# Graph layer with gathered rows: gather indices for eight blocks in one transfer, in a ring of 16 blocks

## The chip, the core and the metric

The kernel runs on one core of a Trainium2 chip. The core has TensorE (PE, with its weight loads PEld), VectorE (DVE), ScalarE (ACT), GpSimd (POOL), SyncE (SP) and 16 DMA engines. The metric is the time of one execution on the device in microseconds (us); less is better.

## The reference, cut to what matters

A message-passing layer over 12,500 nodes (64 features) and 412,500 edges, sorted by destination:

```python
h = relu(layernorm(x))
h0 = pe_val @ W0 + b0                      # pe_val: 32 features per edge
t  = gelu(h0) @ W1 + b1
h0 = h0 + (gelu(t) @ W2 + b2)
score = h0 @ W3 + b3                       # 64 per edge
msg  = h[src] * score                      # h[src]: the gather
sums = segment_sum(msg, dst); cnt = segment_sum(1, dst)
out  = x + (sums / max(cnt, 1)) @ Wo + bo
```

## The kernel before

Edges are padded to 403 blocks (`NB`) of 1024 edges, each block 8 tiles (`TILES`) of 128. Setup computes the layer norm of x and writes it to DRAM (`h_rows`), loads the weights, and prepares a table of destinations. Then every engine walks over the blocks in its own loop; semaphores alone order the engines among each other.

For block b, with buffers picked by parity (a for even b, b for odd b) or by ring:

- **SP** issues loads four blocks ahead: `pair` (the edge features for the first product) once `h0_done` says that block b's first product is over, `act_in` (the same features for the last product) once `score_done` says that block b's last product is over. Then, for block b + 8, it waits on `gathered` of block b and issues the load of the gather indices `idx` (L221, one block: 128 partitions of 8 numbers, 4 KB). SP works strictly in order, so the index load of block b + 8 stands behind the wait for `score_done` of block b.
- **POOL** runs `gather_ahead`: wait for `msg_done` of block b (the slot of `rows` is free again), wait for `idx_in` of the slot, then eight indirect DMAs (L309), each of which fetches 128 rows of `h_rows` into `rows`. So POOL may be at most 8 blocks (`G_RING`) ahead.
- **PE** per block, in this order in `steps`: `second(b)` (L404, ps_h1), `first(b+1)` (L398, ps_h0, signals `h0_done`), `sums(b-1)` (L422, ps_w, after `msg_done` of b-1), `last(b)` (L413, ps_s, signals `score_done`). The names ps_sa and ps_sb tell even blocks from odd ones.
- **ACT** applies gelu twice: `g` from ps_h0 (L353), then `act_in` from ps_h1 (L358).
- **DVE** builds the one-hot tile (L574), then `message(b)` (L582) multiplies ps_s with `rows` after it has waited for `score_done` and `gathered` of block b, signals `msg_done`, and adds a window of sums into `acc` (L684).

The wait of POOL on the indices and the load that answers it are:

```python
slot = s % G_RING
pool.wait_ge(idx_in[slot], uses(b, G_RING) * 16)
...
sp.wait_ge(gathered[s % G_RING], uses(b, G_RING) * 16 * TILES)
load_idx(b + G_RING, s + G_RING)
```

Of the kernel before, what the change touches and what calls it, by code (L numbers as in the profile page):

```python
# [22 lines left out]
I32 = mybir.dt.int32  # L23
# [4 lines left out]
P = 128  # L28
# [4 lines left out]
TILES = 8  # L33
HALF = TILES // 2 * P
BLOCK = TILES * P
NB = -(-E // BLOCK)
# [12 lines left out]
G_RING = 8  # L49
IN_RING = 4  # L50
# [18 lines left out]
def edge_gated_layer(nc, x, edges, src, dst, dst_rows, weights, out):  # L69

    with ExitStack() as ctx:
        def sb(name, shape, dt=F32):
            return ctx.enter_context(nc.sbuf_tensor(name, shape, dt))
# [4 lines left out]
        def sem(name):  # L78
            return ctx.enter_context(nc.semaphore(name))
# [32 lines left out]
        iota_i = sb("iota_i", [P, WIN], I32)  # L112
        iota = sb("iota", [P, WIN])

        idx = sb("idx", [P, G_RING, TILES], I32)
        pair = sb("pair", [2 * DE, IN_RING, HALF])
        act_in = sb("act_in", [D + DE + 1, IN_RING, 2, HALF])
        g1 = sb("g1", [P, 2, HALF])
# [38 lines left out]

        pair_in = [sem(f"pair_in{s}") for s in range(IN_RING)]
        attr_in = [sem(f"attr_in{s}") for s in range(IN_RING)]
        idx_in = [sem(f"idx_in{s}") for s in range(G_RING)]  # L160
        gathered = [sem(f"gathered{s}") for s in range(G_RING)]
        h0_done = sem("h0_done")
        g1_done = sem("g1_done")
# [6 lines left out]
        msg_done = sem("msg_done")  # L170
# [25 lines left out]
        def blocks_loop(eng, first, end, unroll, step):  # L196

            turns = (end - first) // unroll
            if turns < 2:
                turns = 0  # L200
            else:
                with eng.Fori(0, turns) as i:
                    for u in range(unroll):
                        step(i * unroll + (first + u), first + u)
            for b in range(first + turns * unroll, end):
                step(b, b)

        def uses(b, ring):

            return (b >> ring.bit_length() - 1) + 1  # L210

        def tiles_of(b):
            return LAST_TILES if isinstance(b, int) and b == NB - 1 else TILES
# [3 lines left out]

        @block.sync
        def _(sp):
            def load_idx(b, s):  # L220
                sp.dma_start(idx[:, s % G_RING, :], src[one(b), :, :].rearrange("o p t -> p (o t)")  # L221
                             ).then_inc(idx_in[s % G_RING], 16)

            def load_pair(b, s):
                sp.dma_start(pair[:, s % IN_RING, :],
                             edges[one(b), :, :, :].rearrange("o g f j -> (o g f) j")
                             ).then_inc(pair_in[s % IN_RING], 16)

            def load_attr(b, s):
                sp.dma_start(act_in[D:D + DE, s % IN_RING, :, :],  # L230
                             edges[one(b), :, :, :].rearrange("o g f j -> f (o g) j")
                             ).then_inc(attr_in[s % IN_RING], 16)

            load_idx(0, 0)
            load_idx(1, 1)
            for c in range(LN_STEPS):
                cols = slice(c * LN_ROWS, (c + 1) * LN_ROWS)
                sp.dma_start(xs[:, cols, :], x_nodes[:, cols, :]).then_inc(x_in[c], 16)
            for b in range(2, G_RING):
                load_idx(b, b)  # L240
            sp.dma_start(wp[:, :], weights).then_inc(weights_in, 16)
            for b in range(2):
                load_pair(b, b)
                load_attr(b, b)
            sp.dma_start(dst_i[:, :, :], dst).then_inc(dst_in, 16)
            for c in range(CHUNKS):
                n = len(range(c, NB, CHUNKS))
                if c >= 2:

                    sp.wait_ge(bounds_step, 1 + 2 * (c - 1))  # L250
                sp.dma_start(rows_i[0:n, c % 2, :], dst_rows[c:NB:CHUNKS, :]
                             ).then_inc(rows_in[c % 2], 16)
            for b in range(2, IN_RING):
                load_pair(b, b)
                load_attr(b, b)
            sp.dma_start(x_late[:, :, :], x[N_EARLY:N, :].rearrange("(t p) d -> p t d", p=NP)
                         ).then_inc(x_late_in, 16)

            sp.wait_ge(bounds_step, 1 + 2 * CHUNKS)
            sp.dma_start(bounds_dram.rearrange("m (p c) -> p m c", p=P), bounds[:, :, :]  # L260
                         ).then_inc(bounds_out, 16)
            sp.wait_ge(bounds_out, 16)
            sp.dma_start(base_b[:, :], bounds_dram[0:1, 0:NB].broadcast_to([P, NB])
                         ).then_inc(base_in, 16)
            sp.dma_start(top[:, :], bounds_dram[1:2, 0:NB]).then_inc(base_in, 16)

            def ahead(b, s):

                sp.wait_ge(h0_done, b + 1)
                load_pair(b + IN_RING, s + IN_RING)  # L270

                sp.wait_ge(score_done, b + 1)
                load_attr(b + IN_RING, s + IN_RING)

            def ahead_all(b, s):
                ahead(b, s)

                sp.wait_ge(gathered[s % G_RING], uses(b, G_RING) * 16 * TILES)
                load_idx(b + G_RING, s + G_RING)

            blocks_loop(sp, 0, NB - G_RING, G_RING, ahead_all)
            for b in range(NB - G_RING, NB - IN_RING):
                ahead(b, b)


            for half in range(2):
                k0, k1 = half * len(groups) // 2, (half + 1) * len(groups) // 2
                c0, c1 = groups[k0][0], sum(groups[k1 - 1])
                sp.wait_ge(y_ready, k1)
                sp.dma_start(y_nodes[:, c0:c1, :], ln_y[:, c0:c1, :]).then_inc(y_out, 16)  # L290
            sp.wait_ge(y_ready, len(groups) + 1)
            sp.dma_start(out[N_EARLY:N, :].rearrange("(t p) d -> p t d", p=NP), y_late[:, :, :]
                         ).then_inc(y_out, 16)
            sp.wait_ge(y_out, 16 * 3)
            sp.wait_ge(h_out, 16 * LN_STEPS)


        @block.gpsimd
        def _(pool):
            pool.iota(iota_i[:, :], pattern=[[1, WIN]], base=0, channel_multiplier=0  # L300
                      ).then_inc(set_up, 1)

            def gather(b, s, table):
                slot = s % G_RING
                pool.wait_ge(idx_in[slot], uses(b, G_RING) * 16)

                pool.sem_inc(gathers_begun, 1)
                for t in range(tiles_of(b)):
                    pool.indirect_dma_start(  # L309
                        rows[:, slot, t, :], None, table,  # L310
                        bass.IndirectOffsetOnAxis(ap=idx[:, slot, t:t + 1], axis=0),
                    ).then_inc(gathered[slot], 16)

            for b in range(RAW):
                gather(b, b, x)

            pool.wait_ge(h_out, 16 * LN_STEPS)
            for b in range(RAW, G_RING):
                gather(b, b, h_dram)

            def gather_ahead(b, s):

                pool.wait_ge(msg_done, b + 1)
                gather(b + G_RING, s + G_RING, h_dram)

            blocks_loop(pool, 0, NB - G_RING, G_RING, gather_ahead)


        @block.scalar
# [419 lines left out]
def one(b):  # L749

    return bass.ds(b, 1)
# [52 lines left out]
```

## Time and profile before

| | |
|---|---|
| median of 3 runs | 5398.31 us (5397.2 to 5401.39) |
| span of the profiled execution, first to last instruction | 5345.7 us |
| TensorE, share of the span busy | 70% |
| GpSimd, share of the span busy | 58% |
| VectorE, ScalarE | 13%, 18% |
| mean granted TensorE clock | 0.517 of full speed |

The page gives the profiled execution as its span alone; the median of the runs lies 52.6 us above that span, which is the time around the first and the last instruction. Busy shares are averages over the span. For every instruction the trace gives its start, its length, the idle time of its engine before it, and what ended that idle time (behind the arrow); "remote" stands for a release that the profile could not put down to a recorded instruction.

### The profile page before, as it was taken

To read this page: it belongs to the slowest core of one execution; us is meant where nothing else is said; L and a number is where in the kernel's file an instruction comes from. 1 tells how busy PE (TensorE), PEld (TensorE's weight loads), DVE (VectorE), ACT (ScalarE), POOL (GpSimd) and SP (SyncE) were. 2 spreads that over 40 slices of the span, in tenths; PEclk is the share of its full clock that TensorE was granted. 3 is DMA by queue.
4 is the path that set the end of the run, shared out by engine and by line. 5 is a ranking of instruction groups with operands and counts; after the bars stand their busy time and mean duration, and the time that the engine had idled before them with its cause. 6 is when DMAs were issued, how large, how long until landed. Compare 5 with 4: busy or idle time off the path is not lost.

```text
span 5345.7 us, 46327 instructions
## 1 busy us (share of the span) xinstructions
PE 3746.6 (70%) x14718; PEld 2524.4 (47%) x14719; DVE 710.2 (13%) x1345; ACT 986.2 (18%) x1329; POOL 3080.2 (58%) x3228
## 2 busy tenths in 40 slices
PE   0677667777677777677776677776777767777678
PEld 0444444444444444444444444444544444444456
DVE  3211111111111111111111111111111111111112
ACT  2211111111111111111111111111111111111111
POOL 5655555555555555555555555555555555555551
PEclk9655555555555555555555555555555555555555
DMA  3111111111111111111111111111111111111111
GB/s 105 39 41 40 41 41 41 42 40 41 41 42 40 43 41 41 40 42 42 41 40 41 41 41 42 41 41 40 42 43 40 40 41 42 42 40 40 41 36 43
DMA packets 229106, 226.99 MB, mean 42 GB/s; under 512 B 123910, under 2 KB 124039, under 8 KB 228722
## 3 DMA queue, kind: packets, MB, share of 16 engines
q0 software_dynamic: 103136, 105.82, 10.8%
q1 hardware_dynamic: 125434, 117.78, 7.6%
q10 hardware_dynamic: 520, 3.20, 0.1%
q8 instruction: 8, 0.13, 0.0%
q14 instruction: 8, 0.07, 0.0%
HBM read 220.11 MB, written 6.40 MB: 42 GB/s over the span
## 4 chain that ended last, share of the span: by engine, by line
another core or an unknown queue 66%; PE 22%; DVE 4%; issue 3%; DVEq 3%; DMA 1%; ACT 1%; SPq 0%; ACTq 0%
PE ps_sa L413 12%; PE ps_wb L422 7%; DVE msg L582 3%; DVEq L679 2%; DVEq L581 1%; DMA rows_i<-in_dst_rows 1%; PE ps_sb L413 0%; PE ps_h1a L451 0%; PE ps_h1b L451 0%; DVE acc L684 0%; PE ps_wa L422 0%; DVE hot L574 0%; DMA xs<-in_x 0%; DVEq L684 0%
## 5 line engine op out<-in xcount | busy, mean ns | idle before, releaser
L309 POOL DMA_INDIRECT rows<-h_rows,idx x3175 | 3026.4, 953 | 2174.9 <-DMA idx<-in_src 1226.2
L422 PE MATMUL ps_wb<-hot,msg 128*65 128x64 f32 x3216 | 404.1, 318 | 1399.0 <-DVE msg L582 1389.7
L422 PEld LDWEIGHTS ps_wb<-hot,msg 128*65 128x65 f32 x3216 | 367.0, 228 | 1712.5 <-DVE msg L582 1687.4
L358 ACT ACTIVATE act_in<-ps_h1a,wp 64x512 f32<-64x512 f32 x404 | 276.1, 683 | 2972.6 <-remote 2847.2
L413 PE MATMUL ps_sa<-w_last,act_in 97*128 97x64 f32 x3232 | 726.8, 419 | 71.2 <-DVE w_last L608 69.2
L413 PEld LDWEIGHTS ps_sa<-w_last,act_in 97*128 97x128 f32 x3232 | 709.0, 331 | 73.3 <-DVE w_last L608 70.8
L413 PE MATMUL ps_sb<-w_last,act_in 97*128 97x64 f32 x3216 | 726.3, 420 | 2.8 <-issue 1.5
L413 PEld LDWEIGHTS ps_sb<-w_last,act_in 97*128 97x128 f32 x3216 | 708.5, 332 | 3.3 <-issue 1.8
L582 DVE TENSOR_TENSOR msg<-ps_sb,rows 128x512 f32<-128x512 f32 x201 | 139.0, 692 | 3434.0 <-remote 3386.3
L422 PEld LDWEIGHTS ps_wa<-hot,msg 128*65 128x65 f32 x3230 | 369.1, 228 | 336.9 <-issue 295.2
L358 ACT ACTIVATE act_in<-ps_h1b,wp 64x512 f32<-64x512 f32 x402 | 274.6, 683 | 1135.3 <-issue 554.5
L422 PE MATMUL ps_wa<-hot,msg 128*65 128x64 f32 x3230 | 406.9, 319 | 37.2 <-DVE msg L582 36.7
L404 PE MATMUL ps_h1a<-g,wp 128*128 128x512 f32 x404 | 407.1, 1111 | 17.2 <-ACT g L353 12.6
L398 PE MATMUL ps_h0a<-pair,wp 64*128 64x512 f32 x404 | 416.6, 1133 | 0.0
L404 PE MATMUL ps_h1b<-g,wp 128*128 128x512 f32 x402 | 404.5, 1109 | 16.4 <-ACT g L353 15.7
L398 PE MATMUL ps_h0b<-pair,wp 64*128 64x512 f32 x402 | 414.5, 1132 | 1.5 <-issue 1.5
L574 DVE TENSOR_TENSOR hot<-dst_i,iota 128x512 f32<-128x512 f32 x403 | 277.9, 690 | 16.1 <-issue 16.1
L582 DVE TENSOR_TENSOR msg<-ps_sa,rows 128x512 f32<-128x512 f32 x202 | 139.7, 691 | 974.6 <-PE ps_sa L413 899.3
L398 PEld LDWEIGHTS ps_h0b<-pair,wp 64*128 64x128 f32 x402 | 100.0, 308 | 302.8 <-issue 302.8
L398 PEld LDWEIGHTS ps_h0a<-pair,wp 64*128 64x128 f32 x404 | 100.4, 308 | 301.3 <-issue 301.2
L353 ACT ACTIVATE g<-ps_h0a,wp 128x512 f32<-128x512 f32 x202 | 138.8, 687 | 123.4 <-issue 75.0
L353 ACT ACTIVATE g<-ps_h0b,wp 128x512 f32<-128x512 f32 x201 | 138.2, 687 | 6.2 <-issue 1.2
(63 smaller groups left out, 714.2 us busy)
## 6 DMA issues: line engine op xcount, KB each, us to landing
pair<-in_edges SPq DMA_DIRECT2D x403, 128.0 KB
act_in<-in_edges SPq DMA_DIRECT2D x403, 128.0 KB
rows<-h_rows,idx POOLq DMA_INDIRECT x3175
idx<-in_src SPq DMA_DIRECT2D x403, 4.0 KB
xs<-in_x SPq DMA_DIRECT2D x4, 781.2 KB
h_rows<-ln_d ACTq DMA_DIRECT2D x4, 781.2 KB
dst_i<-in_dst SPq DMA_DIRECT2D x1, 1612.0 KB
out<-ln_d SPq DMA_DIRECT2D x1, 1530.0 KB
```

What stands on the lines that cost most here:

```text
L309: pool.indirect_dma_start(rows[:, slot, t, :], None, table, bass.IndirectOffsetOnAxis(ap=idx[:, slot, t:t + 1], axis=0),).then_inc(gathere ...
L353: act.activation(g1[:, s % 2, :], ps_h0[s % 2][:, :], ACT.Gelu, bias=b0).then_inc(g1_done, 1)
L358: act.activation(act_in[0:D, s % IN_RING, g, :], ps_h1[s % 2][g * D:(g + 1) * D, :], ACT.Gelu, bias=wp[g * D:(g + 1) * D, C_B1:C_B1 + 1]). ...
L398: pe.matmul(ps_h0[s % 2][:, :], w0, pair[:, s % IN_RING, :], start=True, stop=True).then_inc(h0_done, 1)
L404: pe.matmul(ps_h1[s % 2][:, :], w1, g1[:, s % 2, :], start=True, stop=True).then_inc(h1_done, 1)
L413: mm = pe.matmul(ps_s[s % 2][:, t * D:(t + 1) * D], act_in[:, s % IN_RING, g, j * P:(j + 1) * P], w_last[:, :], start=(t == 0), stop=(t == ...
L422: last = pe.matmul(window, msg[:, s % 2, t, :], onehot[:, t, :], start=(t == 0), stop=(t == n - 1))
L574: return dve.tensor_tensor(to, rel.unsqueeze(2).to_broadcast([P, TILES, WIN]), iota_tiles, ALU.is_equal)
L581: dve.wait_ge(gathered[s % G_RING], (uses(b, G_RING) - 1) * 16 * TILES + 16 * n)
L582: dve.tensor_tensor(msg[:, s % 2, 0:n, 0:D], ps_s[s % 2][:, 0:n * D].rearrange("p (t d) -> p t d", d=D), rows[:, s % G_RING, 0:n, :], ALU. ...
L679: base = dve.value_load(base_b[0:1, one(b)], min_val=0, max_val=N - 1)
```

## The change

One index load now brings the indices of eight blocks (a "group") into one half of a ring of 16 blocks. There are two semaphores `idx_in`, one for each half. POOL waits for indices at the first block of each group only. SP issues the load of group g + 2 after the eight `ahead` steps of group g and a wait for `msg_done` of its last block. POOL's loop is unrolled over 16 blocks in place of 8, SP's loop over two groups. At the start the first group's load stands before the loads of x and the second group's behind them.

```diff
-        idx = sb("idx", [P, G_RING, TILES], I32)
+        idx = sb("idx", [P, 2, G_RING, TILES], I32)
...
-        idx_in = [sem(f"idx_in{s}") for s in range(G_RING)]
+        idx_in = [sem(f"idx_in{h}") for h in range(2)]
...
-            def load_idx(b, s):
-                sp.dma_start(idx[:, s % G_RING, :], src[one(b), :, :].rearrange("o p t -> p (o t)")
-                             ).then_inc(idx_in[s % G_RING], 16)
+            def load_idx(group, half, n=G_RING):
+
+                sp.dma_start(idx[:, half, 0:n, :],
+                             src[bass.ds(group * G_RING, n), :, :].rearrange("b p t -> p b t")
+                             ).then_inc(idx_in[half], 16)
...
             load_idx(0, 0)
-            load_idx(1, 1)
             for c in range(LN_STEPS):
                 cols = slice(c * LN_ROWS, (c + 1) * LN_ROWS)
                 sp.dma_start(xs[:, cols, :], x_nodes[:, cols, :]).then_inc(x_in[c], 16)
-            for b in range(2, G_RING):
-                load_idx(b, b)
+            load_idx(1, 1)
...
-            def ahead_all(b, s):
-                ahead(b, s)
-
-                sp.wait_ge(gathered[s % G_RING], uses(b, G_RING) * 16 * TILES)
-                load_idx(b + G_RING, s + G_RING)
-
-            blocks_loop(sp, 0, NB - G_RING, G_RING, ahead_all)
-            for b in range(NB - G_RING, NB - IN_RING):
+            GROUPS = -(-NB // G_RING)
+            TURNS = GROUPS // 2 - 1
+
+            def group_ahead(group, half):
+
+                for u in range(G_RING):
+                    ahead(group * G_RING + u, u)
+
+                sp.wait_ge(msg_done, group * G_RING + G_RING)
+                load_idx(group + 2, half)
+
+            with sp.Fori(0, TURNS) as i:
+                for half in range(2):
+                    group_ahead(i * 2 + half, half)
...
             def gather(b, s, table):
-                slot = s % G_RING
-                pool.wait_ge(idx_in[slot], uses(b, G_RING) * 16)
+                slot, half = s % G_RING, s // G_RING % 2
+                if slot == 0:
+                    pool.wait_ge(idx_in[half], (uses(b, 2 * G_RING)) * 16)
...
-                        bass.IndirectOffsetOnAxis(ap=idx[:, slot, t:t + 1], axis=0),
+                        bass.IndirectOffsetOnAxis(ap=idx[:, half, slot, t:t + 1], axis=0),
...
-            blocks_loop(pool, 0, NB - G_RING, G_RING, gather_ahead)
+            blocks_loop(pool, 0, NB - G_RING, 2 * G_RING, gather_ahead)
```

What it moves on POOL, at the head of the loop over blocks (the gathers of blocks 8 and 9), before:

```order
L305 ISA [waits msg_done]
L309 DMA rows<-h_rows,idx 128x64 [waits idx_in0]
L309 DMA rows<-h_rows,idx 128x64 x7
L323 REGISTER_ALU
L305 ISA [waits msg_done]
L309 DMA rows<-h_rows,idx 128x64 [waits idx_in1]
```

and in the changed kernel at the same place:

```order
L317 ISA [waits msg_done]
L321 DMA rows<-h_rows,idx 128x64 [waits idx_in1]
L321 DMA rows<-h_rows,idx 128x64 x7
L335 REGISTER_ALU
L321 DMA rows<-h_rows,idx 128x64 [waits msg_done]
```

The first block of a group still has both waits; each of the seven others has the wait for `msg_done` alone.

On SP, one block of the loop before (`pair`, `act_in`, then the wait on `gathered` and the index load):

```order
L225 ISA [waits h0_done]
L225 DMA pair<-in_edges 64x512
L230 DMA act_in<-in_edges 32x2x512 [waits score_done]
L278 ISA
L221 ISA [waits gathered0]
L221 DMA idx<-in_src 128x8
```

and in the changed kernel the last block of a group, which is the one that has an index load:

```order
L227 ISA [waits h0_done]
L227 DMA pair<-in_edges 64x512
L232 DMA act_in<-in_edges 32x2x512 [waits score_done]
L222 ISA [waits msg_done]
L222 DMA idx<-in_src 128x8x8
```

Seven of eight blocks on SP now end with the `act_in` load; in the eighth the index load waits for the message of that same block.

## Rows read from the trace of the kernel before

**Rows 1.** The page: busy time of each engine, and slices of POOL and clock.

```profile
PE 3746.6 (70%) x14718; PEld 2524.4 (47%) x14719; DVE 710.2 (13%) x1345; ACT 986.2 (18%) x1329; POOL 3080.2 (58%) x3228
...
POOL 5655555555555555555555555555555555555551
PEclk9655555555555555555555555555555555555555
```

**Rows 2.** Waits over the whole span: total us, times, longest us.

```profile
POOL rows L309 <- DMA idx<-in_src: 1235.1, 198, 46.3
```

**Rows 3.** Waits from 400 to 5100 us: total us, times, longest us.

```profile
DVE msg L582 <- remote: 3207.9, 182, 18.1
ACT act_in L358 <- remote: 2716.0, 182, 15.3
...
PE ps_wb L422 <- DVE msg L582: 1327.3, 180, 7.8
POOL rows L309 <- DMA idx<-in_src: 1092.3, 181, 6.5
POOL rows L309 <- issue: 837.4, 2737, 3.3
```

**Rows 4.** Timeline of one steady cycle: start us, us, engine, line, operation.

```profile
2584.51 0.95 POOL L309 DMA_INDIRECT rows<-h_rows,idx  x1 [6.07 <-DMA idx<-in_src]
...
2593.23 3.62 PE L413 MATMUL ps_sb<-w_last,act_in 97*128 97x64 f32 x16
...
2596.64 2.02 PE L404 MATMUL ps_h1a<-g,wp 128*128 128x512 f32 x2
...
2603.26 0.95 POOL L309 DMA_INDIRECT rows<-h_rows,idx  x1 [0.30 <-issue]
...
2607.34 0.32 SPq L230 DMA_DIRECT2D act_in<-in_edges  x1
2607.39 1.39 ACT L358 ACTIVATE act_in<-ps_h1a,wp 64x512 f32<-64x512 f32 x2 [15.18 <-remote]
2607.52 0.69 DVE L582 TENSOR_TENSOR msg<-ps_sb,rows 128x512 f32<-128x512 f32 x1 [17.89 <-remote]
2608.00 0.35 SPq L221 DMA_DIRECT2D idx<-in_src  x1
...
2610.08 3.62 PE L413 MATMUL ps_sa<-w_last,act_in 97*128 97x64 f32 x16
...
2610.40 0.96 POOL L309 DMA_INDIRECT rows<-h_rows,idx  x1 [6.19 <-DMA idx<-in_src]
...
2613.91 0.69 DVE L582 TENSOR_TENSOR msg<-ps_sa,rows 128x512 f32<-128x512 f32 x1 [4.64 <-PE ps_sa L413]
```

**Rows 5.** Timeline of the start: block 4's last product, and its message.

```profile
166.85 1.95 PE L413 MATMUL ps_sa<-w_last,act_in 97*128 97x64 f32 x16
...
189.06 0.94 POOL L309 DMA_INDIRECT rows<-h_rows,idx  x1 [0.30 <-issue]
193.37 0.69 DVE L582 TENSOR_TENSOR msg<-ps_sa,rows 128x512 f32<-128x512 f32 x1 [27.23 <-remote]
```

**Rows 6.** Timeline: the one place where POOL waited for a message last.

```profile
132.82 0.69 DVE L582 TENSOR_TENSOR msg<-ps_sa,rows 128x512 f32<-128x512 f32 x1
134.44 0.94 POOL L309 DMA_INDIRECT rows<-h_rows,idx  x1 [31.14 <-DVE msg L582]
```

**Rows 7.** Timeline of an odd cycle, in which POOL's pause was short.

```profile
3795.70 0.95 POOL L309 DMA_INDIRECT rows<-h_rows,idx  x1 [3.29 <-issue]
...
3800.43 0.69 DVE L582 TENSOR_TENSOR msg<-ps_sa,rows 128x512 f32<-128x512 f32 x1 [6.23 <-PE ps_sa L413]
...
3804.07 0.69 ACT L353 ACTIVATE g<-ps_h0a,wp 128x512 f32<-128x512 f32 x1 [0.61 <-issue]
...
3805.78 3.62 PE L413 MATMUL ps_sb<-w_last,act_in 97*128 97x64 f32 x16
...
3818.49 0.69 DVE L582 TENSOR_TENSOR msg<-ps_sb,rows 128x512 f32<-128x512 f32 x1 [16.31 <-remote]
```

**Rows 8.** The page: index loads issued, with their size.

```profile
idx<-in_src SPq DMA_DIRECT2D x403, 4.0 KB
```

More of the change, by code:

```diff
@@ L273, in ahead @@
                 load_attr(b + IN_RING, s + IN_RING)
-            def ahead_all(b, s):
-                ahead(b, s)
-                sp.wait_ge(gathered[s % G_RING], uses(b, G_RING) * 16 * TILES)
-                load_idx(b + G_RING, s + G_RING)
-            blocks_loop(sp, 0, NB - G_RING, G_RING, ahead_all)
-            for b in range(NB - G_RING, NB - IN_RING):
+            GROUPS = -(-NB // G_RING)
[8 more added lines that the diff above has]
+                    group_ahead(i * 2 + half, half)
+            for group in range(TURNS * 2, GROUPS - 2):
+                for u in range(G_RING):
+                    ahead(group * G_RING + u, u)
+                sp.wait_ge(msg_done, group * G_RING + G_RING)
+                load_idx(group + 2, group % 2, min(G_RING, NB - (group + 2) * G_RING))
+            for b in range((GROUPS - 2) * G_RING, NB - IN_RING):
                 ahead(b, b)
```

## The prediction

> **What bounds the kernel now.** I began with the shares of the page [rows 1]: no engine is near full, PE at 70%, POOL at 58%, so the time is set by engines that wait for each other. POOL's slices lie even over the whole span, and the granted clock stands at 5 tenths from the second slice on, which is the 1.2 GHz level. So one cycle, repeated, tells the time. The waits from 400 to 5100 us [rows 3] have two totals that belong together: 182 times DVE's message of an odd block (ps_sb) waits for something "remote", 3207.9 us in all, and 181 times POOL waits for indices, 1092.3 us or 6.03 us each. Twice 182 blocks in 4700 us make a cycle of two blocks of 4700 / 182 = 25.8 us, 12.9 us per block.
>
> The timeline of one cycle [rows 4] shows how it turns. POOL starts at 2584.51 and issues 16 gathers, two blocks, at 1.25 us each (0.95 us and a gap of 0.30), until 2604.21. PE does the last product of the odd block from 2593.23 to 2596.85 and the next product (ps_h1a) until 2598.66. Yet SP, ACT and DVE, all of which wait for signals of PE (`score_done`, `h1_done`), go on only at 2607.34, 2607.39 and 2607.52: more than 10 us after PE's record ends. They go on together, about 3.1 us after POOL's last gather ended. The same stands at the start [rows 5]: block 4's last product ended at 168.80, POOL gathered on until 190.00, and the message came at 193.37, 3.4 us after it. I read this as a hold: a signal of PE that becomes due late in a burst of gathers arrives only when the burst is over and has drained. The trace doesn't say why; it shows it in nearly every cycle. The even block's signal, due 3.3 us into the burst (2613.70 against 2610.40), passes at once: its message starts at 2613.91.
>
> So the cycle is a ring of three parts: a burst of 16 gathers, 19.7 us; the drain until the release, 3.1 us here; and the time from the release, 2607.33, to POOL's next gather, 2610.40, 3.1 us. A burst ends because the next slot of `rows` and the next indices both hang on the odd block's held `score_done`.
>
> **What the change takes from the ring.** Before, SP gets `score_done`, issues the `act_in` load at 2607.34, the index load at 2608.00, and POOL gathers at 2610.40 [rows 4]. Side by side with it, DVE's message runs from 2607.52 to 2608.21, and POOL would be free to go then. The change takes the index load out of this place: the indices of group g + 2 are asked for after group g, a whole group before POOL needs them. That is eight blocks, some 100 us, against the 2.4 us that a load took from issue to use. What is late next is the message, and it is not far behind.
>
> How long POOL takes from a message's end to its gather is in one row [rows 6]: the message ends at 133.51, the gather starts at 134.44, 0.93 us. There the indices were in already. The lower bound is the gap of 0.30 us that POOL has between any two gathers. I take 0.93, the row that is the very thing. So POOL would start at 2608.21 + 0.93 = 2609.14 in place of 2610.40, 1.26 us earlier; with 0.30 it would be 1.89 us.
>
> POOL waited for indices 198 times in the whole span [rows 2]. **Sum:** 198 x 1.26 = 249 us off a span of 5345.7 us, that is 5097. By the bound of 0.30 it is 374 us.
>
> Does the rest of the ring stay as it is when POOL starts 1.26 us sooner after the release? PE's work hangs on the release and not on POOL's start, so everything of PE comes 1.26 us later within a burst: the even block's signal 4.6 us in, the odd block's 13.6. The trace has just such a cycle [rows 7]: POOL paused only 3.29 us and started at 3795.70; the even message followed at 3800.43, 4.7 us in, without delay; the gelu that needs the next `h0_done` began 8.4 us in, also prompt; the odd block's last product ended at 3809.40, 13.7 us in, and its message came at 3818.49, held to the end of the burst as ever. So I expect bursts of 16 again, and a cycle of 25.8 - 1.3 = 24.5 us.
>
> **The other parts of the change.** 403 index loads of 4 KB [rows 8] become 51 of 32 KB. One issue took SP 0.35 us [rows 4]; the new one moves the same 1024 short pieces that eight did, so I bound its issue from 0.35 us to 8 x 0.35 = 2.8 us. Behind it on SP stand `pair` and `act_in` loads for blocks four ahead, 50 us before use; that hides either bound. SP's new wait for `msg_done` comes after a wait for the `score_done` of the same block, and the message needs 0.69 us from there. What is queued behind it is again the loads four blocks ahead. If this cover were gone, each group would lose at most that 2.8 + 0.7 us, 50 times, 175 us. At the start the larger first load stands before x: at most 2.8 us once, nothing to 2.8. On POOL seven of eight blocks have one wait less; POOL passed a satisfied wait inside its 0.30 us gap, so that is nothing. I leave these at zero together, and the bound for the groups goes into a rival.
>
> By the Trainium skill, page "DMA: Bandwidth & Descriptors", section "Anatomy of one DMA", a small DMA costs about 2.0 us of fixed time; this case's 2.4 us from SP's issue to POOL's gather is near it. If that whole 2.0 us were saved at each of the 198 waits, the sum would be 396 us; the message beside it is what keeps my term at 1.26 us.
>
> **From the span to the median.** The runs' median 5398.31 lies 52.6 us above the span 5345.7; the change doesn't touch what lies around the span. 5097 + 52.6 = 5149, and I say **5148 us**.
>
> **Rivals.**
> 1. *Longer bursts.* If the odd block's signal slipped through before POOL's second block is issued, POOL would go on for 24 gathers, as it did in [rows 5] with 23. The cycle is then 24 x 1.25 + 3.1 + 1.8 = 34.9 us for three blocks, 11.6 per block against 12.9; over some 390 blocks 500 us, about 4890. For it: a long burst has occurred. Against it: the signal comes later in the burst than before, and [rows 7] shows it still held at 13.7 us. Chance 0.11.
> 2. *The group load costs.* The 1024 pieces of a group's load come in one bunch right after the message of an odd block, which is when POOL starts its next burst. If they hold SP or the first gathers up by up to 3.5 us, 50 times, 175 us of the 249 are lost: about 5320. The trace has no such load. Chance 0.12.
> 3. *Another wait takes the place.* If POOL's start hangs on something else that arrives with the landing of the loads, it stays where it is: 5398, no change. [rows 6] speaks against it, though with a single instance. Chance 0.06.
> 4. *Slower: bursts of one block.* If the even block's signal also fell among the held ones, POOL would stop after 8 gathers, wait for drain and message each time: 9.7 + 3.1 + 1.8 = 14.6 us per block against 12.9, 390 blocks, 660 us more, about 6060. It decides where the even signal comes later than somewhere past 8.4 us into the burst, the latest prompt one in [rows 7]. It will come at 4.6, so there are nearly 4 us to spare; but the hold is a thing I infer and don't understand. A mix with some such cycles would end between. Chance 0.10.
>
> The page "DMA: Bandwidth & Descriptors" of the Trainium skill, section "Specifications", says that pieces under 512 B don't reach line rate. That bears on rival 2; the pieces are as short before as after, 32 B, so by itself it changes no total, only how they are bunched, and no run here shows the price of the bunch.
>
> **How the numbers follow.** My forecast, bursts of 16 with an earlier start, has a chance of 0.61 and its own range 5020 to 5190, from the bound of 0.30 us (374 us) down to 0.93 us with a few cycles disturbed. To hold 8 in 10 the range takes in rival 2 and mixtures with rival 1: 5000 to 5320. Two tenths of a per cent, 11 us, is about what a measurement tells from no change. Faster: 0.61 + 0.11 + 0.12 = 0.84. Same: 0.06. Slower: 0.10.
>
> **What would show it.** In the trace after: the wait of POOL on indices nearly gone and one on DVE's message in its place, some 198 times at 4.8 us (6.03 - 1.26); the message's end to POOL's first gather at 0.9 us; bursts of 16 gathers; a release some 3 us after the last of them; a cycle of 24.5 us. The step on the ring is wrong if the bursts have another length, the step on the price if the pause is not 4.8 us. The prediction falls altogether if the signals are held otherwise than I read it.

## The result, and the profile after

| | before | changed |
|---|---|---|
| median of four runs each | 5399.52 us (5397.2 to 5401.39) | 5173.3 us (5171.89 to 5178.78) |
| ratio | 1 | 0.9583, 95% interval 0.9572 to 0.9594 |
| span of the profiled execution | 5345.7 us | 5171.2 us |

The changed kernel is 226 us faster. The forecast was 5148 us with a range of 5000 to 5320. Around the changed kernel's span lie only 1.9 us (its profiled execution took 5173.1 us). The prediction had taken what lies around the span to be 52.6 us; the section on its steps comes back to that.

The page after: busy time by engine, granted clock, the index loads, the span. Against [rows 1] and [rows 8]: the busy times are nearly the same, on a shorter span.

```profile
span 5171.2 us, 44417 instructions
PE 3760.4 (73%) x14718; PEld 2532.4 (49%) x14719; DVE 710.5 (14%) x1345; ACT 985.8 (19%) x1329; POOL 3098.2 (60%) x3228
PEclk9999999999999999999999999999999999999999
idx<-in_src SPq DMA_DIRECT2D x50, 32.0 KB
```

Waits of the changed kernel from 400 to 5000 us: total us, times, longest us. They answer to [rows 3].

```profile
DVE msg L594 <- remote: 3076.7, 185, 17.3
ACT act_in L370 <- remote: 2534.0, 185, 14.2
PE ps_wa L434 <- DVE msg L594: 1190.6, 184, 7.0
POOL rows L321 <- DVE msg L594: 903.3, 202, 5.2
POOL rows L321 <- issue: 869.5, 2754, 1.0
```

The wait of POOL on indices is gone from the list, and one on DVE's message stands there. The message still waits for "remote" once in two blocks, so what the prediction read as a hold is still there. 185 such waits in 4600 us make a cycle of 24.9 us; it was 25.8.

The timeline of one cycle after, with the columns of [rows 4]. The held block is now an even one (ps_sa); its last product ends at 2600.46, and its message starts at 2609.93. The last row stands 19.7 us behind the index load.

```profile
2580.75 0.94 POOL L321 DMA_INDIRECT rows<-h_rows,idx  x1 [0.30 <-issue]
2584.92 0.33 SPq L232 DMA_DIRECT2D act_in<-in_edges  x1
2585.10 0.69 DVE L594 TENSOR_TENSOR msg<-ps_sa,rows 128x512 f32<-128x512 f32 x1 [16.71 <-remote]
2586.16 0.69 DVE L586 TENSOR_TENSOR hot<-dst_i,iota 128x512 f32<-128x512 f32 x1
2586.58 1.09 POOL L321 DMA_INDIRECT rows<-h_rows,idx  x1 [4.88 <-DVE msg L594]
2591.49 0.69 DVE L594 TENSOR_TENSOR msg<-ps_sb,rows 128x512 f32<-128x512 f32 x1 [4.64 <-PE ps_sb L425]
2592.97 1.10 POOL L321 DMA_INDIRECT rows<-h_rows,idx  x1 [0.30 <-issue]
2596.84 3.62 PE L425 MATMUL ps_sa<-w_last,act_in 97*128 97x64 f32 x16
2600.25 2.02 PE L416 MATMUL ps_h1b<-g,wp 128*128 128x512 f32 x2
2605.61 0.94 POOL L321 DMA_INDIRECT rows<-h_rows,idx  x1 [0.30 <-issue]
2609.75 0.33 SPq L232 DMA_DIRECT2D act_in<-in_edges  x1
2609.80 1.39 ACT L370 ACTIVATE act_in<-ps_h1b,wp 64x512 f32<-64x512 f32 x2 [13.98 <-remote]
2609.93 0.69 DVE L594 TENSOR_TENSOR msg<-ps_sa,rows 128x512 f32<-128x512 f32 x1 [16.68 <-remote]
2611.41 1.09 POOL L321 DMA_INDIRECT rows<-h_rows,idx  x1 [4.85 <-DVE msg L594]
2613.46 0.94 POOL L321 DMA_INDIRECT rows<-h_rows,idx  x1 [0.96 <-issue]
2617.20 0.39 SPq L222 DMA_DIRECT2D idx<-in_src  x1
2619.37 0.01 SPq L227 DMA_DIRECT2D pair<-in_edges  x1
2636.90 0.97 POOL L321 DMA_INDIRECT rows<-h_rows,idx  x1 [5.02 <-DVE msg L594]
```

The ring reads as before, with one part shorter. The burst of gathers: 2586.58 to 2606.55, 16 gathers, 19.97 us (19.70 in [rows 4]). Drain: 2606.55 to 2609.75, 3.20 us (3.13). Turn: the message ends at 2610.62 and the gather starts at 2611.41, 0.79 us later; it had been 2.19 us, from 2608.21 to 2610.40. The gathers at 2586.58 and 2592.97 last 1.1 us where the others last 0.94; DVE's one-hot ran beside the first of them, from 2586.16 to 2586.85. That is where this burst became longer. The next one, in which the index load falls, is longer for another reason too: POOL pauses 0.96 us before its second gather, at 2613.46, in place of 0.30.

### The profile page after: what moved, and what is told of

It reads as the page before. It is cut to its first block, busy times and chain, and to the rows that moved or that the text cites. A ratio compares the mean times of both kernels' runs of the same rounds, so it can differ in the third digit from the quotient of the medians.

```text
span 5171.2 us, 44417 instructions
## 1 busy us (share of the span) xinstructions
PE 3760.4 (73%) x14718; PEld 2532.4 (49%) x14719; DVE 710.5 (14%) x1345; ACT 985.8 (19%) x1329; POOL 3098.2 (60%) x3228
## 4 chain that ended last, share of the span: by engine, by line
another core or an unknown queue 65%; PE 18%; issue 8%; DVE 4%; DVEq 4%; DMA 1%; ACT 0%; SPq 0%; ACTq 0%
PE ps_sb L425 10%; PE ps_wa L434 6%; DVEq L691 2%; DVE msg L594 2%; DVEq L593 1%; DMA rows_i<-in_dst_rows 1%; DVE acc L696 0%; PE ps_sa L425 0%; PE ps_h1a L463 0%; DVE hot L586 0%; DMA xs<-in_x 0%; PE ps_h1b L463 0%; DVEq L696 0%; PE ps_h1a L416 0%
## 5 line engine op out<-in xcount | busy, mean ns | idle before, releaser
L416 PE MATMUL ps_h1b<-g,wp 128*128 128x512 f32 x402 | 406.2, 1113 | 19.2 <-ACT g L365 15.7
L410 PE MATMUL ps_h0a<-pair,wp 64*128 64x512 f32 x404 | 418.7, 1138 | 0.4 <-issue 0.4
L410 PE MATMUL ps_h0b<-pair,wp 64*128 64x512 f32 x402 | 416.5, 1138 | 0.0
```

The source lines that it names most:

```text
L410: pe.matmul(ps_h0[s % 2][:, :], w0, pair[:, s % IN_RING, :], start=True, stop=True).then_inc(h0_done, 1)
L416: pe.matmul(ps_h1[s % 2][:, :], w1, g1[:, s % 2, :], start=True, stop=True).then_inc(h1_done, 1)
```

## The experiments

**A finding ahead of them.** The experiments ran in four sessions, on three chips, each beside the kernel before. In three of the four the kernel before took about 4255 us, not 5399: there the profiles show no signal of PE that is held. In the last it took 5398.76 us (5396.53 to 5401.69). It isn't the chip's number: one and the same number gave 4255 us in one session and 5399 in another. I call these an *unheld* and a *held* place. Each ratio below is to the kernel before on the same chip at the same time. Except for the last, all experiments ran in unheld places.

### Early index loads without grouping

A ring of 16 single index slots, each block's load issued 16 blocks ahead; the rest as before. It was meant to tell "early" from "grouped".

```diff
-        idx = sb("idx", [P, G_RING, TILES], I32)
+        idx = sb("idx", [P, 2 * G_RING, TILES], I32)
...
-                load_idx(b + G_RING, s + G_RING)
+                load_idx(b + 2 * G_RING, s + 2 * G_RING)
```

> The kernel before, with one part of the change alone: a ring of 16 index slots, but still one index load of 4 KB and one wait on indices per block; the load is for the block 16 ahead, so its landing lies 100 us before its use. Theory (the landing of the indices stood on the ring between the release and POOL's next burst): the same as the changed kernel, 5173 us within 20 us, POOL's pause between bursts about 4.9 us and ended by DVE's message. Rival (what counts is that there is one transfer and one wait in eight blocks): 5400 us, as before.

Measured: 4252.47 us, ratio 0.9993 (0.9984 to 1.0003). The place was unheld, so there was no ring to shorten, and neither theory was tested. The timeline, DVE and POOL only:

```profile
1999.73 0.69 DVE L582 TENSOR_TENSOR msg<-ps_sb,rows 128x512 f32<-128x512 f32 x1 [8.59 <-DMA rows<-h_rows,idx]
1999.76 0.95 POOL L309 DMA_INDIRECT rows<-h_rows,idx  x1 [0.30 <-issue]
2000.78 0.69 DVE L574 TENSOR_TENSOR hot<-dst_i,iota 128x512 f32<-128x512 f32 x1
2001.01 1.28 POOL L309 DMA_INDIRECT rows<-h_rows,idx  x1 [0.30 <-issue]
```

POOL gathers without a pause, and the message waits for the landing of rows: POOL is the bound here. The row at 2001.01 shows something else: a gather beside the one-hot takes 1.28 us, one beside the message 0.95. The same kernel a second time:

> Single index loads in a ring of 16, as in the first run of it. Where the kernel before takes 5400 us: by my theory 5173 us within 20 us, by the rival (one transfer and one wait in eight blocks is what counts) 5400 us. Where it takes 4255 us: the same as before, as measured.

Measured: 4252.15 us, ratio 0.9992 (0.9983 to 1.0002). The place was again unheld.

### A pause of POOL after each block

The changed kernel, in which POOL also waits for each block's own gathers.

```diff
                     ).then_inc(gathered[slot], 16)
+                pool.wait_ge(gathered[slot], (uses(b, G_RING) - 1) * 16 * TILES + 16 * tiles_of(b))
```

> The changed kernel, in which POOL after the 8 gathers of each block waits until they have landed. That adds a pause of about 2.2 us (1.4 us of landing, 0.8 us until the next gather) in the middle of each burst of 16. If a held signal of TensorE needs some 3 us without gathers to come through, the pause frees nothing: a cycle of 11.9 + 9.7 + 3.3 + 1.6 = 26.5 us for two blocks and about 5500 us. If any pause after landing frees it, the bursts become 8 gathers long and the block takes 11.9 us: about 4950 us.

Measured: 4968.41 us, ratio 1.1674 (1.1654 to 1.1693). With nothing held, the pauses of about 2.3 us a block are plain loss: 12.1 us a block against 10.3 in the changed kernel without them. Whether a pause would free a held signal stays unanswered.

### Plain copies in place of gathers

Both leave the gather out: `rows` is filled by copies of fixed rows. In the first POOL issues them, from block 6 on; in the second SP issues them for all blocks, and POOL issues none.

```diff
+                        pool.dma_start(rows[:, slot, t, :], h_dram[t * P:(t + 1) * P, :]
+                                       ).then_inc(gathered[slot], 16)
```

> The changed kernel, which from block 6 on copies eight fixed runs of 128 consecutive rows per block in place of gathering by index; the copies are issued by POOL on the same queue, of the same bytes and number. It leaves the gather out. Theory A (the hold comes from POOL writing the descriptors of its transfers): the hold stays, messages of every other block wait 'remote', between 4700 and 5250 us depending on what a copy costs POOL. Theory B (it comes from scattered reads or from the indirect form): the hold is gone and TensorE's own 9.2 us per block set the time, 3900 to 4050 us.

```diff
+                    sp.dma_start(rows[:, slot, t, :], table[t * P:(t + 1) * P, :]
+                                 ).then_inc(gathered[slot], 16)
```

> As the kernel with plain copies from POOL, but the copies are issued by SP on its hardware queue (all blocks, the first six from x); POOL has no transfer at all. It leaves the gather out. Theory A (POOL's descriptor writing is what holds TensorE's signals): no hold, no 'remote' waits, TensorE nearly without a pause at 9.2 us per block, 3900 to 4100 us. Rival (the bytes that land in SBUF, or the number of completions, hold the signals): every other message is still late and the time stays above 4700 us.

Measured, by POOL: 2201.81, 3884.87, 2201.70 and 3891.97 us. By SP: 3882.61, 3890.62, 3750.79 and 3247.33 us. The place was unheld and would have shown no hold with the gathers either, so they don't separate the theories. They show what is next: TensorE, which was busy for all of the middle stretch. In the two profiled runs the time goes with its speed; of the other six no profile was kept. One group of the first, profiled at 2201.8 us, and the same group of the second, profiled at 3882.6 us (busy us, mean ns of one, idle before):

```profile
L429 PE MATMUL ps_sa<-w_last,act_in 97*128 97x64 f32 x3232 | 404.0, 279 | 69.6 <-DVE w_last L624 69.3 <-ACT act_in L374 0.2
```

```profile
L434 PE MATMUL ps_sa<-w_last,act_in 97*128 97x64 f32 x3232 | 728.7, 420 | 63.1 <-DVE w_last L629 63.1
```

### The changed kernel once more

No edit.

> The changed kernel itself, once more. In the four runs before this one the kernel before took 4255 us and no signal of TensorE was held, so what the change is worth may depend on where the kernel runs. If the kernel before takes about 4255 us here as well, POOL gathers without a pause and the landing of the indices is hidden: the changed kernel is the same within 0.3%. If the kernel before takes about 5400 us here, the hold is there and the ratio is 0.958 again. A rival says that the gain is one of the change and not of the place: 0.958 in either case.

Measured: 4254.15 us against 4254.7, ratio 0.9999 (0.999 to 1.0009). The waits from 400 to 4000 us:

```profile
DVE msg L594 <- DMA rows<-h_rows,idx: 2964.3, 350, 8.7
```

Every message waits for its rows and POOL for nothing. Where signals aren't held, the change is worth nothing.

### The hold written in by hand

To test the ring in an unheld place, the hold was put into the program: for each odd block b, SP before its `act_in` load and DVE before its message also wait until the gathers of block b + 7 have landed, which is the end of the burst. This was added to the kernel before, to the changed kernel, and to the ring of 16 single slots.

```diff
                 sp.wait_ge(score_done, b + 1)
+                if s % 2 == 1 and (not isinstance(b, int) or b + 7 < NB - 1):
+                    sp.wait_ge(gathered[(s + 7) % G_RING], uses(b + 7, G_RING) * 16 * TILES)
                 load_attr(b + IN_RING, s + IN_RING)
...
+                if s % 2 == 1 and (not isinstance(b, int) or b + 7 < NB - 1):
+                    dve.wait_ge(gathered[(s + 7) % G_RING], uses(b + 7, G_RING) * 16 * TILES)
```

> The hold written into the kernel before, where none is by itself: for every odd block b, SP (before the act_in load) and DVE (before the message) also wait until the gathers of block b + 7 have landed, which is the end of POOL's burst. Theory: the ring of the slow executions comes back, a burst of 16 gathers (20.3 us), 1.4 us of landing, 3.0 us from there to POOL's next gather with the index load in it: 24.7 us for two blocks against 20.6 us, so 4255 + 200 x 4.1 = 5075 us. The waits of POOL end on the indices. This kernel is the base for the next two.

> The same two waits written into the changed kernel. Theory (the change is worth the index landing minus the message beside it, once for each burst): POOL's pause is 1.4 + 1.5 us, 23.2 us for two blocks, 4255 + 200 x 2.6 = 4775 us, 0.94 of the kernel before with the same waits. Rival (the landing of the indices is no part of the ring; the gain came from something else of the place where it was measured): within 1% of the kernel before with the same waits.

> The same two waits written into the kernel with single index loads and a ring of 16. Theory: what counts is that the load is early, not that it is one for eight: like the changed kernel with the waits, 4775 us, at most 25 us more for the wait per block that POOL still has. Rival (fewer transfers and waits are what counts): like the kernel before with the waits, 5075 us.

| with the hold written in | us | ratio to the kernel before without it |
|---|---|---|
| kernel before | 5079.99 | 1.1938 (1.1918 to 1.1958) |
| changed kernel | 4828.82 | 1.1348 (1.1329 to 1.1367) |
| ring of 16 single loads | 4840.44 | 1.1375 (1.1356 to 1.1394) |

The turn of the ring in the kernel before with the hold:

```profile
2012.68 0.69 DVE L586 TENSOR_TENSOR msg<-ps_sb,rows 128x512 f32<-128x512 f32 x1 [16.22 <-DMA rows<-h_rows,idx]
2013.18 0.35 SPq L221 DMA_DIRECT2D idx<-in_src  x1
2015.79 0.94 POOL L311 DMA_INDIRECT rows<-h_rows,idx  x1 [4.78 <-DMA idx<-in_src]
```

and in the changed kernel with the hold:

```profile
2009.11 0.69 DVE L598 TENSOR_TENSOR msg<-ps_sb,rows 128x512 f32<-128x512 f32 x1 [14.94 <-DMA rows<-h_rows,idx]
2010.58 0.94 POOL L323 DMA_INDIRECT rows<-h_rows,idx  x1 [3.12 <-DVE msg L598]
```

The first is the turn of [rows 4] once more, the second that of the cycle after. From the message's start to the gather it is 3.11 us and 1.47 us. The change takes 5079.99 to 4828.82 us, 4.9% off, against 4.2% where the chip holds the signals itself; a steady cycle falls from 24.42 to 23.14 us. The first time met its expectation of 5075; the second is 54 us above the 4775 expected, though its cycle is the 23.2 us of the expectation. So a signal that comes only at the end of a burst is enough to make the change pay, and taking the index load out of the turn is what pays. The third row of the table separates early from grouped: early single loads get 239.6 of the 251.2 us, and the grouping 11.6 us more. Here a group load does not cost; it saves a little.

The same runs settle a rival for the hold itself: that the rhythm of 16 gathers and a pause makes it. ACT has no wait written in, and it does not wait for rows. In the changed kernel with the hold written in, the burst started at 2010.58, and a signal of PE that was due 15.7 us later passed at once:

```profile
2024.27 2.02 PE L418 MATMUL ps_h1a<-g,wp 128*128 128x512 f32 x2
2026.32 1.39 ACT L372 ACTIVATE act_in<-ps_h1a,wp 64x512 f32<-64x512 f32 x2 [6.49 <-PE ps_h1a L418]
```

From 400 to 4600 us all 182 signals of this kind passed within 0.04 us. In the changed kernel of the result the 169 that were due 15 us into a burst came 7.2 to 8.1 us late, as ACT's row at 2609.80 above (due 2602.27). So the rhythm alone does not hold a signal.

### The one-hot's second operand in PSUM

The gather of 1.28 us beside the one-hot suggests a way to speed POOL up. In the changed kernel the row of column numbers (`iota`) goes to the spare columns of the two `ps_w` banks, so that the one-hot reads one operand in SBUF and one in PSUM.

```diff
-            dve.tensor_copy(iota[:, :], iota_i[:, :]).then_inc(set_up, 1)
+            dve.tensor_copy(ps_w[0][:, WIN:2 * WIN], iota_i[:, :])
+            dve.tensor_copy(ps_w[1][:, WIN:2 * WIN], iota_i[:, :]).then_inc(set_up, 1)
...
-            iota_tiles = iota[:, :].unsqueeze(1).to_broadcast([P, TILES, WIN])
+            iota_tiles = [ps_w[k][:, WIN:2 * WIN].unsqueeze(1).to_broadcast([P, TILES, WIN])
+                          for k in range(2)]
```

> The changed kernel, with the row of numbers that the one-hot comparison reads kept in a free part of the sums' PSUM banks, so that this comparison of VectorE reads one operand from SBUF in place of two. Where POOL gathers without a pause, a block takes it 10.28 us, of which 8 x 1.25 = 10.0 are gathers; the gather that runs beside the comparison is 0.3 us longer. Theory (the two readers meet at a port that VectorE and GpSimd share): every gather takes 0.95 us and a block 9.95 us, so 4255 - 403 x 0.33 = 4122 us. Rival (the gather is longer there for another reason, for instance the message or SP's loads): no change, 4254 us.

Measured: 4142.99 us, ratio 0.9738 (0.9721 to 0.9754). It is the fastest of the kernels that compute the whole reference, faster than the kernel before and the changed one; it ran in an unheld place only. The expectation was 4122 us: a block takes 0.28 us less, from 10.27 to 9.99, not 0.33. In its timeline a gather starts inside the one-hot, as it did at 2001.01 above, and takes 0.94 us:

```profile
2017.71 0.69 DVE L588 TENSOR_TENSOR hot<-dst_i,ps_wb 128x512 f32<-128x512 f32 x1
2017.88 0.94 POOL L321 DMA_INDIRECT rows<-h_rows,idx  x1 [0.30 <-issue]
```

All gathers together, in the changed kernel in its unheld run and then in this one (busy us, mean ns of one, idle before):

```profile
L321 POOL DMA_INDIRECT rows<-h_rows,idx x3175 | 3120.1, 983 | 1013.2 <-issue 966.0
```

```profile
L321 POOL DMA_INDIRECT rows<-h_rows,idx x3175 | 3007.3, 947 | 1011.2 <-issue 966.1
```

They take 3120.1 - 3007.3 = 113 us less, and the kernel takes 4254.15 - 4142.99 = 111 us less, as it should where POOL is the bound.

### Three kinds of copy in one kernel

Blocks up to 135 are gathered by POOL as in the changed kernel; from 136 to 263 POOL issues plain copies of fixed rows; from 264 on SP does. From block 136 on the gather is left out. So one execution shows in its own first stretch whether its place holds.

```diff
+                    if table is None:
+                        pool.dma_start(rows[:, slot, t, :], h_dram[t * P:(t + 1) * P, :]
+                                       ).then_inc(gathered[slot], 16)
...
+            blocks_loop(pool, 0, PLAIN_POOL - G_RING, 2 * G_RING, gather_ahead)
+            blocks_loop(pool, PLAIN_POOL - G_RING, PLAIN_SP - G_RING, 2 * G_RING, copy_ahead)
```

> Three ways to fill the rows in one execution of the changed kernel: blocks to 135 gather by index on POOL, blocks 136 to 263 have fixed runs of rows copied by POOL, blocks from 264 on have them copied by SP. From block 136 on it leaves the gather out. Where TensorE's signals are held with gathers: if POOL's writing of descriptors is the cause, they are held in the second stretch too and free in the third (9.2 us per block or less); if scattered reads or the indirect form are the cause, they are free in the second stretch as well; if the landing bytes are, they are held in all three. Where nothing is held: 10.3 us per block in the first stretch, set by POOL, and 9.2 us or less in the others.

Measured: 3970.23 us, one run, in an unheld place: 10.27 us a block with gathers and 9.18 with either copy, where PE is the bound. Then the same kernel again, in the place that proved to be a held one:

> The kernel with three ways to fill the rows, once more, because the kernel before took 4255 us on each of the three chips that ran so far (from block 136 on it leaves the gather out). If the kernel before takes about 5400 us here, the three stretches show what holds TensorE's signals: POOL's own transfers (held in the first two), the indirect form (held in the first alone), or the landing bytes (held in all). If it takes 4255 us, the stretches take 10.28, 9.18 and 9.18 us per block again and the cause of the hold stays open.

Measured: 4304.34 and 4289.92 us, ratio 0.7959 (0.7926 to 0.7992). Waits of three stretches, 400 to 1700, 1900 to 2800 and 2900 to 4100 us:

```profile
DVE msg L630 <- remote: 862.8, 52, 17.2
ACT act_in L401 <- remote: 710.3, 52, 14.1
...
POOL rows L347 <- DVE msg L630: 253.2, 62, 5.1
```

```profile
POOL rows L344 <- DVE msg L630: 467.2, 98, 5.1
DVE msg L630 <- PE ps_sb L456: 365.0, 49, 7.6
```

```profile
DVE msg L630 <- PE ps_sb L456: 482.8, 65, 7.6
DVE msg L630 <- PE ps_sa L456: 479.4, 65, 7.6
```

And the three windows (busy us of PE, PEld, DVE, ACT, POOL; granted clock, DMA share, GB/s):

```profile
400.00:1700.00 1300.00, 965.43 (x3777) 647.19 (x3776) 159.62 (x313) 249.04 (x341) 801.74 (x838) 0.50 0.19 43
1900.00:2800.00 900.00, 900.00 (x3530) 604.86 (x3528) 149.93 (x294) 233.72 (x320) 415.04 (x785) 0.50 0.21 58
2900.00:4100.00 1200.00, 1200.00 (x4713) 807.46 (x4712) 198.84 (x390) 311.21 (x426) 3.67 (x7) 0.50 0.23 58
```

"Remote" and the 16 to 17 us waits belong to the gathers alone: 12.43 us a block, then 9.18 and 9.18. The DMA share is no lower in the later stretches, so the bytes that land in `rows` are not what holds PE's signals. Nor is it enough that POOL issues transfers:

```profile
2201.75 4.23 POOL L344 DMA_DIRECT2D rows<-h_rows  x8 [4.94 <-DVE msg L630]
```

But these copies come in bursts of 4.2 us, since a plain copy takes POOL 0.53 us and a gather 1.25, and POOL then pauses for 4.9 us. Whether it is the indirect gathers or the length of POOL's unbroken work that holds the signals is not separated.

## Why the prediction was right, and where it was off

- **The ring and its release: right.** The bursts are of 16, the release comes some 3 us after the last gather, and the even-and-odd pattern stayed. One reading was loose: not all of SP, ACT and DVE went on more than 10 us after PE's record ended. For ACT, whose product ended at 2598.66, it was 8.7 us; the hold is there all the same. That a hold at the burst's end turns the index load into lost time was shown by writing such a hold in: the cost and the gain both appeared in a place that has no hold of its own.
- **The term of 1.26 us a burst: mis-sized.** It was made of a turn of 0.93 us from the message's end to the gather [rows 6]; it measured 0.79 us in the timeline. Over the steady cycles of both profiled executions, from 400 to 5000 us, message start to gather start fell from 2.98 to 1.51 us, which is 1.47 us. Two things that the prediction took as unchanged gave part of it back. From the last gather's end to the message it is 3.37 us in place of 3.04; no run shows why. And the burst is 20.02 us in place of 19.77. Of this 0.09 us are longer gathers: 228 in 184 bursts took over 1 us, against 80 in 178, each of them begun while DVE's one-hot ran. The kernel with the one-hot's operand in PSUM shows that this pairing stretches gathers, in an unheld place. The other 0.16 us are POOL's pause of 0.96 us before the second gather, in every fourth burst; no run shows its cause. The net is 0.89 us a cycle, some 178 us over 200 cycles; the two profiled spans differ by 174.5 us. With the hold written in, where the wait after the last gather stayed at 1.66 us, the cycle fell by 1.28 us, close to the 1.26 forecast.
- **The 52.6 us around the span: wrong.** The prediction said that the runs' median lies 52.6 us above the span 5345.7, and that the change doesn't touch what lies around it. Around the span lie 2 us: another execution of the kernel before, at 5396.53 us, has a span of 5394.6. No time is on record for the profiled execution of [rows 1]; if 2 us lie around it too, it was some 50 us shorter than the usual one. The forecast of the span, 5097, missed 5171.2 by 74 us; the added 52.6 covered most of that, so that 5148 came within 26 us of the median is in part luck. Between medians the change is worth 226 us, 1.1 us a cycle, against the 249 and 1.26 forecast. What the usual execution spends that the profiled one did not is open.
- **The distance of the load: wrong, without harm.** The prediction had the indices asked for a whole group, some 100 us, before their use. But SP's load waits for the last message of group g, and POOL's first gather of group g + 2 needs only the message after that one. So in the steady stretch the load left 19.4 to 19.8 us before the gather that needs it (2617.20 and 2636.90 above), with the hold written in 11.0 us. Both are well over the 2.4 us that a load took.
- **The parts taken as zero: nearly right.** The group's load took SP 0.39 us to issue, and the next load left at 2619.37, 2.2 us after the load had started, inside the bound of 2.8 us. From 400 to 5000 us no engine's list of waits names `idx` or `pair`. But the 46 cycles in which a group's load falls took 25.35 us, the other 138 took 24.75: 0.60 us each, some 30 us over 50 loads.
- **Rival 1 and rival 4 (bursts of 24 or 8)** did not occur: every steady burst of the profiled execution is 16 gathers long. **Rival 2 (the group load costs)** did not occur at its price: with the hold written in, grouped loads beat single ones by 11.6 us. Where the chip holds the signals, single early loads were not timed; there the cost is at most the 30 us above, not 175, and the longer pause in those cycles begins before the load leaves. **Rival 3 (another wait in its place)** is refuted by POOL's pause, 4.88 us where it had been 6.0; the forecast was 4.8.
- **What the prediction had no case for:** in a place where no signal is held, the same change is worth nothing, ratio 0.9999. "The prediction falls altogether if the signals are held otherwise than I read it" named the condition; that it differs between places was not thought of.

Open stay why one place holds PE's signals and another doesn't, and which property of the gathers does it. The shown part is that the hold belongs to the stretch with gathers on POOL, that the rhythm of the bursts alone does not make it, and that the change is worth 1.1 us a cycle between the medians.

## What to carry to other kernels

When an engine waits for a small load in every turn of a ring, ask the load earlier, and price the gain by the next thing that it waits for, not by the load's whole time: here that was the message, 0.69 us long, and 0.79 us from its end to the gather. The worth of such a load hangs on the ring being the bound, so time the change on more than one chip and occasion; if an engine waits for "remote" there and for recorded work elsewhere, one and the same edit is worth 4% or nothing. And where GpSimd is the bound, look for VectorE operations that read two SBUF operands beside it.

## What the runs showed of the hardware

- The same kernel takes 4255 us or 5399 us, by place and time. Where it takes 5399, the engines that wait for signals of PE due late in a burst of 16 gathers on POOL go on some 3 us after the burst's end (3.20 us in the timeline after).
- An indirect gather of 128 rows took POOL 0.94 us, and 1.28 us when it began while the one-hot with both inputs in SBUF ran (0.46 us of the one-hot lay inside it). Of 299 gathers that began so in the changed kernel's unheld run, from 400 to 3900 us, 298 took over 1 us; the 60 that had begun before the one-hot took 0.94. Beside the message, which reads PSUM and SBUF, it took 0.95. With one input of the one-hot moved to PSUM it was 0.94 again. By the Trainium skill, page "SBUF — State Buffer", section "🔬 SBUF: two separate sides", a VectorE operation with two SBUF inputs and a GpSimd operation that reads SBUF exclude one another. The stretch and its cure agree with that for the gather; a one-hot that began during a gather still took 0.69 us.
- The granted clock of the record doesn't tell TensorE's speed alone. In the changed kernel the page shows 9 tenths, the level of 2.4 GHz, and in the kernel before 5 tenths, that of 1.2 GHz [rows 1]; yet the first product took 1138 ns in both. Runs of the changed kernel recorded at 0.999 and at 0.517 took 5173.1 and 5171.89 us. The first product's group from 400 to 5000 us (busy us, mean ns of one, idle before), before and after:

```profile
L398 PE MATMUL ps_h0a<-pair,wp 64*128 64x512 f32 x356 | 368.8, 1138 | 0.0
```

```profile
L410 PE MATMUL ps_h0a<-pair,wp 64*128 64x512 f32 x370 | 383.3, 1138 | 0.0
```

- With plain copies by POOL the last product's matmuls took 279 ns each and the kernel 2201.8 us; with copies by SP 420 ns and 3882.6 us. Where the gather is no longer the bound, TensorE's speed decides, and it differed from run to run.
